# Four full tiles of the second expert layer planned from three groups' lists and taken beside the last group's router and lists

## The reference

```python
xt = layernorm(x).reshape(-1, 256)               # 2048 rows
top_vals, top_idx = top_k(xt @ gate_w.T, 2)      # the router
combine = one_hot(top_idx) weighted by softmax(top_vals)
h = silu(xt @ w1[e].T) * (xt @ w3[e].T)          # for the chosen experts e
y = sum over e of combine[:, e] * (h @ w2[e].T)
x = x + y
```

## Time and profile before

| what | us |
|---|---|
| median of 3 runs (1640.03 to 1643.32) | 1642.14 |
| the profiled execution's own time | 1637.2 |
| its span, first to last instruction | 1635.4 |
| PE busy | 1319.6 (81%) |
| DVE busy | 826.0 (51%) |
| ACT busy | 443.3 (27%) |
| mean granted clock of PE, share of full speed | 0.872 |

### The profile page before, as it was taken

One profiled execution on the slowest core, in us unless ns is written; L12 is line 12 of the kernel. 1 busy time (PEld: TensorE's weight loads), 2 busy tenths in 40 slices (PEclk: granted clock), 3 DMA queues, 4 the chain that ended last, 5 costly groups with the idle time before them and its releaser, 6 DMA issues. The chain is left out here.

```text
span 1635.4 us, 25718 instructions
## 1 busy us (share of the span) xinstructions
PE 1319.6 (81%) x8174; PEld 1079.3 (66%) x8186; DVE 826.0 (51%) x2325; ACT 443.3 (27%) x1122; POOL 286.9 (18%) x307
## 2 busy tenths in 40 slices
PE   5877587686479897999887877777369999999997
PEld 3554454453358677888765655555269999999996
DVE  2239868768876775212337576665612222222222
ACT  2635235235222332111232222322111111111111
POOL 2000021021020001000233353432411111111111
PEclk9687677678769998999988988888679999999998
DMA  9993032032075477888300101000178888888884
GB/s 342 351 291 106 1 121 82 0 126 76 0 267 187 157 271 247 296 291 294 106 26 14 39 28 35 29 28 0 52 286 303 316 324 310 313 309 324 319 312 151
DMA packets 116318, 291.52 MB, mean 178 GB/s; under 512 B 8192, under 2 KB 90528, under 8 KB 101024
## 3 DMA queue, kind: packets, MB, share of 16 engines
q1 hardware_dynamic: 106032, 273.00, 47.4%
q0 software_dynamic: 10224, 17.77, 4.2%
HBM read 218.84 MB, written 71.90 MB: 178 GB/s over the span
## 5 line engine op out<-in xcount | busy, mean ns | idle before, releaser
L817 PE MATMUL bank<-norm_cols,work 128*128 128x128 f32 x3488 | 432.4, 278 | 16.4 <-DMA work<-in_moe 9.7
L817 PEld LDWEIGHTS bank<-norm_cols,work 128*128 128x128 f32 x3488 | 422.3, 195 | 30.4 <-issue 17.9
L1737 DVE TENSOR_TENSOR extra<-bank,span 128x256 f32<-128x256 f32 x202 | 85.7, 425 | 391.7 <-ACT span L1529 391.7
L817 PE MATMUL bank<-work,extra 128*128 128x256 f32 x808 | 206.9, 380 | 0.0
L1529 ACT ACTIVATE span<-bank 128x256 f32<-128x256 f32 x202 | 77.4, 383 | 451.6 <-PE bank L817 451.6
L817 PEld LDWEIGHTS bank<-work,extra 128*128 128x128 f32 x808 | 138.6, 191 | 10.7
L2955 POOL DMA_INDIRECT out_x<-att_rows,slot_token x39 | 60.7, 1556 | 377.7 <-ACT att_rows L1539 313.6
L817 PE MATMUL bank<-norm_cols,weights 128*128 128x128 f32 (+2 forms) x416 | 94.4, 388 | 17.3 <-ACT norm_cols L1560 11.0
L2774 POOL TENSOR_TENSOR rstd<-var_eps,neg_half 128x4 f32<-128x4 f32 x18 | 18.3, 1018 | 511.4 <-DVE var_eps L1749 511.4
L817 PE MATMUL bank<-weights,norm_cols 128*128 128x512 f32 (+1 forms) x192 | 89.1, 613 | 8.3 <-ACT norm_cols L1560 5.5
L817 PEld LDWEIGHTS bank<-norm_cols,weights 128*128 128x128 f32 x416 | 69.9, 223 | 35.4 <-ACT norm_cols L1560 16.3
(11 more groups left out here) (349 smaller groups left out, 1982.3 us busy)
## 6 DMA issues: line engine op xcount, KB each, us to landing
work<-in_moe SPq DMA_DIRECT2D x39, 2048.0 KB, 7.8
work<-in_moe SPq DMA_DIRECT2D x70, 1024.0 KB, 9.2
expert_rows_in<-zero SPq DMA_DIRECT2D x3, 5590.0 KB, 46.6
expert_rows_in<-zero SPq DMA_DIRECT2D x3, 5504.0 KB, 36.0
expert_rows_out<-zero SPq DMA_DIRECT2D x3, 5504.0 KB, 22.4
work<-in_moe SPq DMA_DIRECT2D x31, 512.0 KB, 5.7
weights<-in_moe SPq DMA_DIRECT2D x8, 1024.0 KB, 5.5
att_cols<-expert_rows_in SPq DMA_DIRECT2D x39, 130.0 KB, 2.0
```

What stands on the lines that cost most here:

```text
L817: return pe.matmul(o, l, r, start=a, stop=z)
L1737: return dve.tensor_tensor(o, a, b, op)
```

## The change

Two of `phase3`'s gaps on VectorE in the last group get `plan_early_counts(EARLY3)` and `plan_early_tiles(3)`: the first `EARLY3 = 4` full tiles, planned from the lists of groups 0 to 2. SP, after the scatter of group 2, loads the rows of tiles 0 and 1 and the weights of tile 0 at once, and the weights of tile 1 after the last group's x is stored. VectorE keeps the facts of tile 0 and copies its turned rows ahead of `add_out(0)`. PE does the ups of tile 0, and then the last group's router (`last_router`); its `list_ranks` follows the first up of tile 1. VectorE's list work and `plan_tiles` stand between the gates of tiles 0 and 1. The planner's scratch moves from `SPAN` to `NA` and `CG2`. The whole count of tiles stays 39: 4 early and 35 planned later.

```diff
+EARLY3 = 4
+    def with_router(keys, h):
+        at = keys.index(("up", 0, h - 1)) + 1
+        return keys[:at] + [("xT7", 0), ("xT7", 1), ("lg1",), ("up", 1, 0), ("rk",)] + keys[at + 1:]
...
-    j3l = bp.phase(pairs("xT7") + [("lg1",), ("rk",)], 1, None, SIDE)
...
@@ SP, pair(...)
+                    if layer == 3 and plan is start:
+                        filled(plan, turn, ("up", 1, h - 1))
+                        load_up(1, 2 * i + 3)
+                        filled(plan, turn, ("acc", "y", 0))
+                        load_down(0, 2 * i + 2)
+                        filled(plan, turn, ("xsT", 0))
+                        info_kept(0, i + 2)
+                        sp.wait_ge(sem("tiles_planned"), 2)
+                        sp.wait_ge(sem("rows_sent"), 16 * 2 * TILES * 2)
+                        load_rows(0, 2 * i + 4)
+                        return
@@ SP, experts(3)
+                    sp.wait_ge(sem("early_planned"), 2)
+                    filled(j3e, 0, ("o4", STREAMS - 1))
+                    load_rows(0, 0)
                     load_up(0, 0)
+                    load_rows(1, 1)
                     load_down(0, 0)
-                    sp.wait_ge(sem("rows_sent"), 16 * 2 * TILES * 2)
-                    load_rows(0, 0)
-                    load_rows(1, 1)
+                    rows_out(GROUPS - 1)
                     load_up(1, 1)
                     load_down(1, 1)
...
@@ PE
+                if layer == 3:
+                    amid = {("up", 0, HIDS[3] // P // 2 - 1): last_router,
+                            ("up", 1, 0): lambda: list_ranks(start, 0, 2 * GROUPS)}
-            phase3(j3l, 0, GROUPS - 1, None, None, END)
@@ ACT
+                    amid = {("up", 0, HIDS[3] // P // 2 - 1): last_router, ("up", 1, 0): lambda: pair_exp(2 * GROUPS)}
-            router_exps(2 * GROUPS)
@@ DVE, all_experts(3)
+                    def choose():
+                        logits_out(plan, 0)
+                        weights(8)
+                    def weigh():
+                        weights(5)
+                        places(3)
+                    def plan_rest():
+                        places(4)
+                        kept.append(plan_tiles(3))
+                    def rest():
+                        w, j, row = kept[0]
+                        tile_facts(w, j, row, PLACES, TILE_EV[:, EARLY3:MOE_TILES, :])
+                        plan_done()
+                    experts(layer, 0, "start", 0, {("up", 0, 3): choose, ("up", 1, 0): weigh, ("up", 1, 1): lambda: places(4),
+                                                   ("up", 1, 2): plan_rest, ("up", 1, 3): rest})
@@ DVE, phase3
+                else:
+                    plan_early_counts(EARLY3)
                 leaky(0)
                 if following is not None:
                     combine_second(following)
+                else:
+                    plan_early_tiles(3)
                 leaky(1)
...
                 add_mlp(1)
+                if opening is not None:
+                    opening()
                 add_out(0)
...
+            def first_rows():
+                keep_info(0, 0)
+                rows_out(moe[3]["first"][1], 0, 0)
```

More of the change, by code:

```diff
@@ L245, in moe_plan @@
             steps = moe_steps(h, kind)
-            plans[kind] = (steps, bp.phase(moe_keys(steps), turns, 0))
+            keys = moe_keys(steps)
+            if layer == 3 and kind == "start":
+                keys = with_router(keys, h)
+            plans[kind] = (steps, bp.phase(keys, turns, 0, ROUTER_KEYS))
         return plans
@@ L1049, in early_tiles, with experts @@
                     early_down(j)
-            def experts(layer, i, kind, turn, before, before_turn):
+            def experts(layer, i, kind, turn, before, before_turn, amid={}):
                 steps, plan = moe[layer][kind]
@@ L1098, in experts, with last_router @@
                             last.then_inc(bank_full[b], 1)
+                    if s in amid:
+                        amid[s]()
+            def last_router():
+                plan = moe[3]["start"][1]
+                for u in range(STREAMS):
+                    pe.wait_ge(sem(f"out_normed_s{u}"), GROUPS)
+                    ps, b = fill(plan, 0, ("xT7", u))
+                    for c in range(KC):
+                        for t in range(TS):
+                            last = pe.transpose(ps[:, (c * TS + t) * P:(c * TS + t + 1) * P], NX[:, u * TS + t, c * P:(c + 1) * P], ident[:, :])
+                    last.then_inc(bank_full[b], 1)
+                for u in range(STREAMS):
+                    ready(plan, 0, ("xT7", u))
+                logits(plan, 0, "lg1", Wr[3], kT)
             def turned_rows(plan, turn, u, rows):
@@ L1371, in all_experts @@
                 turned_rows(first, 0, 0, XS if layer == 1 else XS3)
-                experts(layer, 0, "start", 0, first, 0)
+                amid = {}
+                if layer == 3:
+                    amid = {("up", 0, HIDS[3] // P // 2 - 1): last_router,
+                            ("up", 1, 0): lambda: list_ranks(start, 0, 2 * GROUPS)}
+                experts(layer, 0, "start", 0, first, 0, amid)
                 loops = LOOPS[layer]
@@ L1520, in router_exps, with experts @@
                 pair_exp(turn)
-            def experts(layer, i, kind, turn):
+            def experts(layer, i, kind, turn, amid={}):
                 steps, plan = moe[layer][kind]
@@ L1539, in experts, with last_router @@
                             act.activation(YS[:, u, :], ps[:, 0:D], ACT.Copy, scale=SLOTW[:, u:u + 1]).then_inc(bank_empty[b], 1)
+                    if s in amid:
+                        amid[s]()
+            def last_router():
+                plan = moe[3]["start"][1]
+                for u in range(STREAMS):
+                    ps, b = full(plan, 0, ("xT7", u))
+                    act.activation(cols_of(kT, u), per_chunk(ps), ACT.Copy).then_inc(bank_empty[b], 1)
+                router_exp(2 * GROUPS)
             def fold_weights():
@@ L2401, in opening @@
                 def opening():
-                    keep_info(0, 0)
-                    rows_out(first, 0, 0)
-                    experts(layer, 0, "start", 0)
+                    plan, turn = moe[3]["start"][1], 2 * GROUPS
+                    weights = Pieces(list_weights(plan, 0, GROUPS - 1, turn, False)).some
+                    places = Pieces(list_places(plan, 0, GROUPS - 1, turn, False)).some
+                    kept = []
+                    def choose():
[13 more added lines that the diff above has]
+                                                   ("up", 1, 2): plan_rest, ("up", 1, 3): rest})
                 straight(opening)
@@ L2420, in combine, with phase3 @@
                 settle()
-            def phase3(plan, turn, g, following, prev=None, before=None):
+            def phase3(plan, turn, g, following, prev=None, before=None, opening=None):
                 streams = range(STREAMS)
```

99 lines of the change are left out of this document (51 added, 48 removed).

## The result

The changed kernel takes 1619.9 us (median of 4 runs, 1615.87 to 1623.8), the kernel before 1641.09 in the same comparison (4 runs, 1637.0 to 1643.32): ratio 0.9878, 95% interval 0.9845 to 0.9911, by this ratio 20.0 us faster (14.6 to 25.4). The forecast was 1623.1, with 1617 to 1629.

A forecast was written before the change was run, and what follows sets the result against it. The loop, with PE always busy, can't shrink, so only its start moves, bound by waits before it. 1197.9 + 1.9 + 1.0 = 1200.8 instead of 1219.84; 1642.1 - 19.0 = 1623.1 us, range 1617 to 1629.

The forecast's parts named there:

- Rows of tile 0: Early load behind group 2's scatter: rows land at 1160.2, with the early plan's 4.4 us on VectorE costed at nothing.
- First weights: Tile 0's 2 MB, issued near 1159.2, land in 7.3 us; the first up starts at 1166.5.
- The last norm: VectorE ahead of the router: 4.8 us later, complete at 1171.0, hidden because PE does four ups first.
- Four ups: Tile 0's ups on PE before the router: 7.3 us, three at low clock, plus 2.0, ending at 1175.8.
- Router and ranks: Last group's router on PE at 2.4 GHz: 1.8 + 1.8 us; ranks add 1.8 together, 1.1 of it waiting.
- The wait at the loop: PE idles 5.9 us before the loop's first product, at 1197.9, for VectorE's copy of tile 2's turned rows.
- The clock: PE at 1.2 GHz after idling: 1.9 us at the loop's start, 1.0 (0 to 2) behind the router.
- Tile 4's weights: Loop's second turn: 2 MB go out at about 1213, arrive at 1221, needed at 1222.4; no loss.
- Sum: Loop's first product at 1197.9 plus 1.9 and 1.0 gives 1200.8 in place of 1219.84: 19.0 us earlier.
- the weights behind the last scatter (2): Rival at the loop's start: the scatter lands late and weights stop PE, 2 to 5 us, 1627; chance 0.12.
- ScalarE's table (3): Rival in the start: a table switch costs twice 1.28 us, the plan comes 1.7 us later, 1624.8; chance 0.07.
- (5): Rival in the loop: each of 37 tiles waits 1.06 us for weights, 39 us against 19 gained, 1662; chance 0.03.

The follow-up runs named there:

- counts_twice: Changed kernel with VectorE counting the full tiles for the early plan twice; ratio 0.9856 to the kernel before.
- rows_behind_norm: Changed kernel with VectorE taking tile 0's turned rows behind the last norm instead of ahead of `add_out(0)`; ratio 0.9868 to the kernel before.
- busy_wait: Changed kernel with 44 unread 128 by 128 products on PE in the wait ahead of the loop; ratio 0.9873 to the kernel before.
- the first trace: The changed kernel's first profiled execution; 458.83 us from the last group's o2 products to the last products.
- the second: The changed kernel profiled once more, unedited; 460.38 us from the last group's o2 products to the last products, ratio 0.9866 to the kernel before.
- copy_first: Changed kernel with VectorE copying tile 2's turned rows ahead of planning the remaining tiles; 1612.06 us, ratio 0.9843 to the kernel before.
- router_first: Changed kernel's early plan and loads, but the last group's router, lists and remaining plan before all products of tile 0; ratio 0.9904 to the kernel before.
- the two edits: On the changed kernel: VectorE's copy ahead of the plan; six early tiles with SP's last-scatter wait two tiles later. Ratios 0.9843 and 0.9864 alone, 0.9828 together.
- weights_first: Changed kernel with SP loading tile 0's 2 MB of weights ahead of its wait for group 2's scatter; ratio 0.9881 to the kernel before.
- six_swap: six_copy_first with tile 0's weights issued ahead of its rows and tile 1's ahead of the store of x; ratio 0.9888 to the kernel before.
- all_three: Changed kernel with the edits of weights_first and six_copy_first together; ratio 0.9855 to the kernel before.
- busy_short: Changed kernel with 22 unread products on PE in the wait ahead of the loop, where busy_wait has 44; ratio 0.9898 to the kernel before.
- six_copy_first: Changed kernel with six early tiles, SP's last-scatter wait two tiles later, and VectorE's copy ahead of the plan; 1610.32 us, ratio 0.9828 to the kernel before.

## Why the prediction was right

Times of this trace, less 2.03, against the prediction's.

- **Rows of tile 0.** Predicted 1160.2; PE starts to turn them at 1159.94. The early plan costs nothing in the end, as said, but it is longer: the counts end 3.0 us after their start, not 1.9, of which 1.1 is one operation that took longer there (below). It does reach PE, which now waits 1.05 us for VectorE ahead of its last products (before it didn't); that is hidden in the wait for the rows. counts_twice shows that even twice as much is hidden.
- **First weights.** Predicted to land in 7.3, first up 1166.5. They took 7.66, first up 1166.71. PE waited 6.08 us for them, the largest wait that is left.
- **The last norm.** Predicted complete at 1171.0, is 1170.5, and hidden: rows_behind_norm.
- **Four ups.** The fourth began 8.05 us after the first instead of 7.3 (the low clock lasted longer; the merged row of the first three has 7.99 us here, 7.02 to 8.44 in the other traces); the router begins at 1176.5, predicted 1175.8.
- **Router and ranks.** Both at full clock, 1.87 to the first logit product and 1.78 for the logits, predicted 1.8 each. The ranks' wait is 1.10, as predicted.
- **The wait at the loop.** Predicted 5.9 us, VectorE's copy last. It is 5.32, of the same cause, and ends at 1198.29 (predicted 1197.9). Plan and end of lists took 6.6 (6.8), slot weights and copy 1.6 (1.6).
- **The clock.** Predicted 1.9 at the loop; 2.25 measured by the loop's distance, 2.33 by busy_wait, 1.4 to 3.3 over six traces. Behind the router I took 1.0 from between 0 and 2. From the first to the third up of tile 1 it was nothing in the first trace, 2.1 in the second, 0.3 to 0.4 in six other runs.
- **Tile 4's weights.** Predicted to go out at about 1213 and to be just in time; issued at 1212.5, no wait. They landed in 8.1 us, at 1222.7 by the trace's own time, and their first product came at 1224.03. The margin of 1.4 us was real and thin: copy_first starts the loop 6 us earlier and waits 3.9 us for weights.
- **Sum.** 19.0 predicted, 19.3 in the first trace, 17.8 in the second. That it fits within 0.3 us is in part luck: the loop's start came 0.4 late and its clock cost 0.35 more, and the 1.0 for the clock behind the router wasn't there. The median came out 3.2 us below the forecast; 4.9 us had been added for the distance of before's median to its profiled run, and after the two agree (1619.9 and 1619.95).
- **The range.** Its terms add up to 5.4 us down and 2.5 up, so 1617.7 to 1625.6; the 1618.5 to 1626 that the prediction gives doesn't follow from them. Only the outer range, 1617 to 1629, was worked out from it.

Of the rivals, the weights behind the last scatter (2) exist, but only for a kernel that starts the loop sooner. ScalarE's table (3): in the start the silu follows its load at once (1183.32 + 1.28) again. Timeline of ScalarE:

```profile
1183.32 1.28 ACT L1563 ACT_TABLE_LOAD   x1
1184.61 0.38 ACT L1563 ACTIVATE span<-bank 128x256 f32<-128x256 f32 x1
```

The second cost that the Trainium skill names (ScalarE: Activation LUTs, What ACT_TABLE_LOAD costs) isn't in these rows either; the trace disagrees with it here. No wait for weights came into the loop (5).

What I hadn't weighed is how the gain is shared: I told the story by the order of PE's work, and router_first shows that the order is worth 1.1 to 2.6 us and the early plan with its loads 16.7.

## What to carry to other kernels

In this kernel early data was worth more than clever order: first ask which loads can be issued before the slow bookkeeping is done, and only then what stands beside it. A wait at a loop's entry that comes from one engine's program order is cheap to remove, but then look for the next bound, here SP's wait in front of the following weights; the two edits gave 0.6 and 1.2 us alone (no more than two traces of one kernel differ) and 6.6 together. A small transfer that others wait for is best issued ahead of a big one (weights_first, six_swap).

## What the runs showed of the hardware

- A small transfer took longer with a big one beside or ahead of it: the last scatter of group 2 landed in 2.44 us alone and in 6.17 beside one 2 MB load (weights_first; 6.37 in all_three); a row load in 2.1 us ahead of 2 MB of weights (changed kernel) and in 7.1 when issued behind them in the same queue (six_swap).
- After a wait of 5.3 us PE starts at 1.2 GHz; with products in the wait it stays at 2.4 (busy_wait), 2.3 us apart. It also started at 1.2 GHz after 3.47 us (copy_first) and 4.04 (weights_first), but not after the 2.85 us of router_first, where the next 16 products took 2.02 us.
- An integer operation on VectorE of 128 x 8 that takes 0.17 us elsewhere took 1.25 to 1.26 at its place in the early counts, in all thirteen traces that have them. GpSimd's addition of 128 x 512 lies over it, and both end at the same time:

```profile
1146.23 1.26 DVE L2294 TENSOR_SCALAR lens_i<-lens_i 128x8 int32<-128x8 int32 x1
```
```profile
1146.20 1.27 POOL L2947 TENSOR_TENSOR work<-work,row_bias 128x512 f32<-128x512 f32 x1 [1.67 <-DVE work L2518]
```

In counts_twice its second instance, with no such addition over it, took 0.17. That GpSimd holds VectorE up is read from this coincidence, not tested alone.
- Stops of PE with nothing shown as their cause, 0.2 to 1.2 us each, in the first turn of the loop (busy_short 3.3 us, six_swap 4.1). six_swap has the PE instructions of six_copy_first, and only SP's order differs, so PE's code alone doesn't make them. What does stays open.
